# Self-attention rounds of a decoder layer: projections, a transpose, the score blocks and the output product in another order on the engines

## The reference

```
q, k, v = heads(x @ Wq + bq), heads(x @ Wk + bk), heads(x @ Wv + bv)    # 16 heads of 8
scores  = where(mask, q k^T / sqrt(8), -inf)     # mask: blocks of 64, and 8 global tokens (rows and columns)
out     = softmax(scores) v @ Wo + bo            # 1. self-attention
...                                              # 2. cross-attention to 64 context rows, then a two-layer MLP
...                                              # 3. 16 experts, top 2 by a router, and a shared expert
```

## Time and profile before

| | us |
|---|---|
| median of 3 runs | 568.07 (563.98 to 569.35) |
| the profiled execution | 568.54 |
| its span | 566.7 |
| self-attention, start-up to the last of its rounds | about 0 to 255 |
| PE busy / DVE / ACT / POOL, whole span | 469.9 / 409.6 / 296.8 / 298.4 |

### The profile page before, as it was taken

The page is one execution under the profiler, slowest core; times in us unless marked ns, Lnnn a source line. Parts: engine busy times, 40 slices in busy tenths (PEclk is TensorE's granted clock), DMA queues, the critical chain, the costliest instruction groups (busy, mean ns, idle before and its releaser), DMA issues. The chain is left out here.

```text
span 566.7 us, 17496 instructions
## 1 busy us (share of the span) xinstructions
PE 469.9 (83%) x6139; PEld 348.1 (61%) x6139; DVE 409.6 (72%) x1247; ACT 296.8 (52%) x757; POOL 298.4 (53%) x588
## 2 busy tenths in 40 slices
PE   1977888888888888888999999999767999999810
PEld 1755666666666666545676676666544888888610
DVE  7566999999888888876889898987572434434337
ACT  2573665555556656524656656564424444444237
POOL 5543454444444334201358888777771577777720
PEclk9997999999999999969999999999989999999975
DMA  6626343455655655326233333332124334333158
GB/s 189 112 51 139 55 71 63 67 132 111 110 108 110 108 107 114 81 52 150 54 83 90 95 87 97 96 85 67 34 97 132 106 110 116 110 109 98 53 178 286
DMA packets 96006, 58.30 MB, mean 103 GB/s; under 512 B 24560, under 2 KB 92224, under 8 KB 95920
## 3 DMA queue, kind: packets, MB, share of 16 engines
q1 hardware_dynamic: 74448, 39.93, 30.2%
q10 hardware_dynamic: 16896, 7.34, 6.7%
q0 software_dynamic: 4576, 9.91, 5.1%
HBM read 20.76 MB, written 17.50 MB: 68 GB/s over the span
## 5 line engine op out<-in xcount | busy, mean ns | idle before, releaser
L507 POOL TENSOR_SCALAR veps<-mv 128x2 f32<-128x2 f32 x48 | 11.2, 232 | 144.9 <-issue 101.2
L1292 ACT ACTIVATE probs<-ps 128x512 f32<-128x512 f32 x128 | 73.3, 603 | 12.1 <-PE ps L1672 9.8
L613 POOL DMA_INDIRECT expert_in<-xn,sloti x64 | 65.5, 1023 | 17.6 <-issue 17.6
L1147 DVE TENSOR_TENSOR eh<-ps,sg 128x256 f32<-128x256 f32 x40 | 17.0, 425 | 59.8 <-ACT sg L1496 58.9
L772 DVE TENSOR_REDUCE nmax<-ps 128x8 f32<-128x512 f32 x64 | 42.5, 686 | 18.9 <-PE ps L1607 18.8
L666 POOL DMA_INDIRECT expert_out<-ey,xt x40 | 38.3, 957 | 27.0 <-DVE ey L1154 16.7
L772 DVE TENSOR_REDUCE mparts<-ps 128x8 bf16<-128x512 f32 x64 | 43.3, 687 | 6.7 <-PE ps L1662 6.3
L1607 PE MATMUL ps<-kbd,qs 96*64 96x128 bf16 x512 | 38.0, 293 | 4.5 <-DMA qs<-part 3.6
L2026 PE MATMUL ps<-wgu,turned 128*128 x160 | 41.3, 380 | 0.0
L1490 ACT COPY turned<-ps 128x512 f32<-128x512 f32 (+1 forms) x43 | 23.8, 554 | 28.5 <-PE ps L2019 23.2
L509 POOL TENSOR_TENSOR rstd<-veps,minus_half 128x2 f32<-128x2 f32 x48 | 35.8, 745 | 4.0
(11 more groups left out here) (248 smaller groups left out, 1360.2 us busy)
## 6 DMA issues: line engine op xcount, KB each, us to landing
kbd<-part SPq DMA_DIRECT2D x192, 32.0 KB
qs<-part ACTq DMA_DIRECT2D x93, 64.0 KB
xt<-expert_in SPq DMA_DIRECT2D x64, 72.0 KB
qs<-part SPq DMA_DIRECT2D x51, 64.0 KB
ck_scr<-wgu SPq DMA_DIRECT2D x6, 512.0 KB
ckbd<-ck_scr SPq DMA_DIRECT2D x16, 192.0 KB
kbd<-part SPq DMA_DIRECT2D x48, 64.0 KB
wgu<-in_L_ffn_gate_up_w SPq DMA_DIRECT2D x4, 512.0 KB, 4.0
```

The costliest lines, as they stand in the source:

```text
L613: pool.indirect_dma_start(xs, bass.IndirectOffsetOnAxis(sloti[b % 3][:, n:n + 1], 0), xn3[b % 3][:, n // TOPK, n % TOPK, :], None).then_in ...
L1292: a_.activation(probs[:, 2 * i:2 * i + 2, :], P2[i % 2][:, :].rearrange("p (j q) -> p j q", j=2), ACT.Exp, scale=SCALE).then_inc(s("probs" ...
```

## The change

In rounds 0 to 13 (`late(b)`), on four engines:

- TensorE: `self_project(b + 2)` goes ahead of `global_query_turn(b)`; the four score blocks follow without a break; `self_out(b - 1)`, `self_global_values(b + 1)` and `global_query_out(b)` follow them. `columns(b + 2)` waits for `x_new`, and `self_out` for `qk32`.
- ScalarE: `self_first_part(b + 2)` and its three DMAs move from the next round's beginning to a place ahead of the odd half of `self_values`; the DMA of piece 2 moves from ahead of `self_columns` to behind it.
- VectorE: `self_last_part` moves behind `shift_spread`, `global_query_max` into `attended`, `global_query_sum` ahead of `stats`, the first `row_max` ahead of `normalise`, `self_end` and `global_heads_out` to the round's end.
- GpSimd: the mask goes ahead of `self_global_columns`. The semaphore `kbg` is merged into `kgqg` (`headed(b)` is its count when the heads of b are laid out).

```diff
@@ gpsimd, self_body
-                if has(b + 2):
-                    self_global_columns(b + 2)
                 if has(b):
                     pool.wait_ge(s_("gexp"), b + 1)
...
+                if has(b + 2):
+                    self_global_columns(b + 2)
@@ vector, self_body
                     shift_spread(b, p, lambda: global_max(b + 1) if has(b + 1) else None)
+                if late(b - 1):
+                    self_last_part(b + 1)
...
-                    attended(b - 1)
...
+                    attended(b - 1, lambda: global_query_max(b) if has(b) else None)
...
+                if late(b):
+                    self_maxima(b + 1, 0, 0)
                 if has(b + 3):
                     normalise(s_, b + 3)
...
-                    if has(b + 2):
-                        self_last_part(b + 2)
+                    if late(b):
+                        if has(b - 1):
+                            self_end(b - 1)
+                        global_heads_out(b)
@@ scalar, self_body
                 if has(b + 1):
-                    self_first_part(b + 1, 1 - p)
-                    if b == 0:
-                        context_rest()
-                    queries_regrouped(b + 1, 1 - p, 0)
+                    if not late(b - 1):
+                        self_first_part(b + 1, 1 - p)
+                        if b == 0:
+                            context_rest()
+                        queries_regrouped(b + 1, 1 - p, 0)
                     self_second_part(b + 1, 1 - p)
-                    if b > 0:
-                        queries_regrouped(b + 1, 1 - p, 2)
...
+                if has(b + 1) and b > 0:
+                    queries_regrouped(b + 1, 1 - p, 2)
                 if has(b):
                     exps(s_, b, (0, 1, 2, 3))
                     global_query_exp(b)
...
                     global_query_norm(b)
+                if late(b):
+                    self_first_part(b + 2, p)
+                    queries_regrouped(b + 2, p, 0)
                 if has(b + 1):
                     self_values(b + 1, 1 - p, (1,))
@@ tensor, self_project and self_out
-                at_least(pe, s_("x_new"), b - 2)
...
+                if late(b + 1):
+                    pe.wait_ge(s_("qk32"), 2 * (b + 3) + 2)
@@ tensor, self_body
+                at_least(pe, s_("x_new"), b - 1)
...
-                if has(b - 1):
-                    self_out(b - 1)
-                if has(b):
+                if late(b):
+                    self_project(b + 2)
                     global_query_turn(b)
-                if has(b + 2):
-                    self_project(b + 2)
...
+                    for half in range(4):
+                        self_scores(b + 1, 1 - p, half // 2, half % 2)
+                    if has(b - 1):
+                        self_out(b - 1)
                     self_global_values(b + 1)
-                    self_scores(b + 1, 1 - p, 0, 1)
-                if has(b):
                     global_query_out(b, p)
```

More of the change, by code:

```diff
@@ L351, in decoder, with late, headed @@
         GOT = {True: 16 * 3 * NP, False: 16 * NP}
+        def late(b):
+            return 0 <= b < B - 2
+        def headed(b):
+            return 3 * b + 2
         def sent_back(q):
@@ L554, in self_global_keys @@
                                          kbd[p][0:KROWS, :, :, :, :].rearrange("p j a k n -> p j a (k n)")[:, :, :, first:first + step * (n - 1) + 1:step])
-                last.then_inc(s_("kbg"), 1)
+                last.then_inc(s_("kgqg"), 1)
             def lay_out_later_stages(b):
-                pool.wait_ge(s_("kgqg"), 2 * b + 4)
+                pool.wait_ge(s_("kgqg"), headed(b + 1))
                 for p in range(2):
@@ L783, in shift_spread, with attended @@
                     v.tensor_copy(qs[p][SHIFT:128, j::2, :], qs[p][SHIFT:128, 0:1, :].to_broadcast([32, PAIRS // 2 - j // 2, S])).then_inc(s_("mT"), 1)
-            def attended(b):
+            def attended(b, between):
                 turned_od = hT[:, :, :].rearrange("p t q -> p (t q)")
@@ L790, in attended @@
                 v.transpose(turned_od, OD[:, :]).then_inc(s_("od_turned"), 1)
+                between()
                 dve.wait_ge(s_("od_turned"), b + 1)
@@ L875, in self_body @@
                     global_rows(b - 1)
+                if has(b):
+                    global_query_sum(b)
                 if has(b + 3):
@@ L879, in self_body @@
                     stats(c_, b + 3 - B, cross_arrived)
-                if has(b):
-                    global_query_sum(b)
-                if has(b - 1):
+                if has(b - 1) and not late(b):
                     self_end(b - 1)
@@ L897, in self_body @@
                     cross_rest(1)
-                self_maxima(b + 1, 0, 0)
+                if not late(b):
+                    self_maxima(b + 1, 0, 0)
                 self_maxima(b + 1, 0, 1)
-                if has(b + 2):
+                if not late(b):
+                    if CROSS and b + 2 == B:
+                        cross_rest(0)
+                    if has(b):
+                        global_heads_out(b)
+                if late(b):
                     self_rest(b + 2, p)
[L902 to L905, removed]
                 self_maxima(b + 1, 1, 0)
@@ L1248, in self_first_part @@
                 act.wait_ge(s_("qk_ps"), 2 * b + 2)
-                at_least(act, s_("kgqg"), 2 * b - 2)
+                at_least(act, s_("kgqg"), headed(b - 2))
                 a_.activation(qk[p][:, 0:S], A0[:, 0:S], ACT.Identity, bias=cols[:, 0:1]).then_inc(s_("qk32"), 1)
@@ L1612, in self_global_scores @@
             def self_global_scores(b, p):
-                pe.wait_ge(s_("kgqg"), 2 * b + 2)
+                pe.wait_ge(s_("kgqg"), headed(b))
                 at_least(pe, s_("probs"), 4 * (b - 1))
@@ L1701, in global_keys @@
                 pe.wait_ge(s_("probs"), 4 * b + 3)
-                pe.wait_ge(s_("kbg"), b + 1)
+                pe.wait_ge(s_("kgqg"), headed(b) + 1)
                 for odd in range(2):
@@ L1756, in self_body @@
                     weigh(s_, b, p, 0, lambda n, j: vbd[p][:, n, j, :], NB)
[L1757 to L1760, removed]
+                if has(b - 1) and not late(b):
+                    if CROSS and b + 2 < B + 2:
                         pe.wait_ge(c_("xnT"), b + 3 - B)
```

33 lines of the change are left out of this document (20 added, 13 removed).

## The result

The change makes the kernel slower: 606.67 us (605.34 to 612.83, 6 runs) against 567.98, a ratio of 1.0714 [1.0677, 1.0752]. The forecast was 612, between 600 and 622. The profiled execution took 612.83 us (span 611.0), 6.2 above the median of its kernel and the slowest of the six; what follows is read from it. If those 6.2 us lie in its 14 changed rounds, which no trace of another execution shows, its rounds are some 0.4 us longer than those of a median run.

What follows compares the result with a forecast made beforehand. TensorE and VectorE were taken to pace the round in turn. A new chain of 16.14 us a round adds 41.7 us over 13 rounds, the fourteenth stretch 2.5; with 568.54, less 0.47, 612 us, range 600 to 622.

Steps and rivals of the forecast that it cites:

- The ring: Closed chain from global scores through VectorE, ScalarE and GpSimd to the next global scores, setting each round at 16.14 us.
- ScalarE standing still behind its issues: ScalarE waits while issuing DMAs: three issues take 1.90 to 2.18 us, taken as 2.04, ahead of the odd values.
- ScalarE hands its DMAs over and goes on: Rival: issues do not hold ScalarE; 2.04, 0.04 and 0.68 leave the chain, 13.4 us a round, 576 us; chance 0.05.
- TensorE and VectorE go on setting the round: Faster rival: the two fullest engines keep pacing the rounds, 0.96 us times 13 come off, 556 us; chance 0.04.
- the occupancy rule: Skill rule judging ScalarE by busy time: work moved ahead there costs nothing, leaving only a gain of 0.96 us a round.
- Its terms: Round's parts through VectorE, ScalarE and GpSimd: 3.02, 3.97, 3.90, 1.48 and 3.77 us, together with the next global scores 16.14.
- then the next global scores: Last step of the round: GpSimd's `qg` releases TensorE's global scores, idle over 1 us for it every round.
- the clock rival: TensorE's granted clock falls too; global scores double by 0.61 us: 620 us in all rounds, 616 in half; chance 0.15.
- Two signs: Right: TensorE idle over 1 us at the global scores every round. Wrong: global scores 0.7 us after the turn.
- The fourteenth stretch: Stretch behind the 13 rounds, old order but late global scores: +2.5 us, between 1.85 and 3.25.
- The third piece: VectorE's part behind the spread, its DMA ahead of ScalarE's exponentials; if ready in time, 0.72 us a round less, 603 us.
- The gain of 0.96 us a round: TensorE's projection ahead of the turn: from turn to first scores 1.23 us before, 0.27 without the projection.

Runs made afterwards that it cites:

- Cutting three links: Changed kernel with ScalarE's three piece-0 issues behind `probs_g`, third piece ahead of the spread, GpSimd's heads ahead of the mask: 586.32 us, ratio 1.0319.
- another order on TensorE and VectorE: Changed kernel with the three mends, first scores ahead of the turn, output product ahead of the last score block, two maxima ahead of normalisation: 565.61 us.
- the first two cuts: Each alone against the changed kernel: ScalarE's three piece-0 issues behind `probs_g`, 598.20 us; VectorE's third piece ahead of the spread, 601.68 us.

## Why the prediction was right, and where not

**The ring is there.** ScalarE standing still behind its issues, read from one row, is one of its links: 13 waits of 27.4 us in the change, and 1.95 us less from the global scores to `probs_g` where the issues move. Cutting three links brought 20.4 of 38.7 us back. "ScalarE hands its DMAs over and goes on" and "TensorE and VectorE go on setting the round" are both out. So is the occupancy rule (the Trainium skill, "Perfetto Trace Analysis", section "Identifying the Most-Contended Engine") as a guide here: ScalarE is busy 7.56 of 16.1 us, and the ring goes through it.

**Its terms**, forecast against the quoted round at the full clock: global scores to exponentials 3.02, measured 2.94; to the projections 3.97, measured 3.69; to the odd values 3.90, measured 3.72; to `probs_g` 1.48, measured 1.48; GpSimd and hand-overs 3.77, measured 3.31. The largest miss is GpSimd's three `kbg` copies, 1.15 us in the row that I summed over and 0.64 now; what made them long before is not settled. Sum 16.14, measured 15.14.

**The step that failed** is "then the next global scores": the ring was to be closed by GpSimd's `qg` in every round, with the clock full. Over the 13 rounds in the trace, global scores to `probs_g` is 12.08 us on average (some rounds have issues of 2.2 to 2.4 us), from there to the last head 3.34, and from there to the next global scores 0.66, where I had 0.05. In eight rounds the heads end 0.56 to 1.54 us ahead, and TensorE, at the lower clock since its waits, is last. That is the clock rival, which I had given 0.15. Its price of 0.61 a round is what the mean comes to (0.66 less 0.05), but not for my reason: the global scores take 0.61 to 0.71 us in the quoted rounds, 0.61 before, and TensorE's work between `pgqT` and them is stretched. The Trainium skill, "TensorE: Matmul & The Clock Gate", section "HAM oscillation", has waits throw the clock back in every round; here it was 11 of 13, and the time was not the 620 of that case. The two rounds at the full clock take 15.14 and 15.66 us from global scores to global scores; the mean is 16.08.

Two signs that I had named came out against me. TensorE was to idle over 1 us for `qg` in every round, and its products did so twice, by up to 0.8. And the global scores 0.7 us behind the turn, a sign of being wrong, are there in five rounds (0.75 to 0.78).

So 16.12 against 16.14 is partly luck: a chain 0.7 too long, a rival left out of the sum, and a trace of the slowest of six executions. By the medians the kernel lost 38.7 us, where the forecast had 44.

**Smaller terms.** The fourteenth stretch: +2.5 forecast, +1.1 measured. Start-up: 0 to 1, measured 1.3. Behind the rounds: nothing, measured 0.5. The third piece, named as the softest term: 603 if it were ready, 9 us less than the sum. When it was ready the time was 601.7, but only 5.0 us less than the change; that the two times meet is luck. The gain of 0.96 us a round from TensorE's order is not shown: with the three links cut and that order kept, the rounds at the full clock take 12.53 and 13.29 us, since TensorE then waits for maxima between the score blocks, a wait that the sum did not have. A gain of 0.4 to 0.6 us a round appears only with another order on TensorE and VectorE.

**Left open:** what the clock's fall alone costs in the change, since no kernel held the clock without other edits; how the 18 us that the three cuts leave divide between TensorE's waits for maxima and the lower clock; and why three issues take 1.85 us in one round and 2.9 in another.

## What to carry to other kernels

An engine's list of DMA issues is work in its order: look at what stands behind an issue and who waits for it, however idle the engine looks. Where moved steps close a ring through several engines, add up the ring, then cut it link by link: the first two cuts gave a third and some four tenths of their length, since the next wait stands right behind, and another order on the fullest engine paid only after all three cuts. A round that gets longer gives TensorE waits, and its stretched tail can take over the end of the ring.

## What the runs showed of the hardware

An issue holds back what stands behind it on ScalarE's list, not what stands ahead of it: with the issues behind the copies, ScalarE's `vbd` copy at 138.90 runs inside the issue of 138.69 to 139.25, and `probs_g` ends 1.48 us after the first of these copies starts, as it did before the change. That issue stands behind `probs_g` on the list and starts 1.02 us ahead of it: "strictly in order", as I wrote of the lists, does not hold between an issue and the instructions ahead of it. In the opposite order the copies wait for all three (1.86 us, then a start 0.05 us after). On the way to `probs_g` the same three issues cost nothing in one order and 1.95 us in the other.

Three issues of 64 KB each took 1.85 to 1.90 us in most rounds, but 2.65 to 2.94 in some of the kernel with the doubled score blocks.
